# Cross-attention and experts on one core: own pair buffers, x normalized in place, expert rows turned by DMA, and a new order on every engine

## The chip, the cores and the metric

The kernel runs on one core of a Trainium2 chip. The metric is the device time of one execution in microseconds; three runs were made before the change (1605.39 median, 1598.07 to 1605.72), and one more execution was taken with the hardware profiler.

## The reference

There are 32 batches of 128 tokens with 512 features. Each batch is normalized, goes through an attention of 32 heads of 16 features, and is added to its input. The result is normalized again and goes through a layer of 8 experts, of which each token takes the best two.

```python
# attention, per batch; adapter = ctx_2048[b], also 128 rows
h = layernorm(x)
q, k, v = split_heads(h @ Wq), split_heads(h @ Wk), split_heads(h @ Wv)
q, k = rope(q), rope(k)
w = softmax(q @ k.T / 4 + mask);  o = w @ v                      # 'own' path
a_k, a_v = split_heads(adapter @ Wk), split_heads(adapter @ Wv)
o += tanh(gate) * softmax(q @ a_k.T / 4) @ a_v                   # 'adapter' path
x = x + o @ Wo
# experts, over all 4096 tokens; H = 512, I = 352, E = 8, K = 2
h = layernorm(x)
topk_vals, topk_idx = top_k(h @ router_w.T, 2);  weight = softmax(topk_vals)
gate, up = split(h[rows of e] @ w1[e].T);  y = (silu(gate) * up) @ w2[e].T
x = x + sum over the two experts of weight * y
```

## The kernel before

The program has two phases with a barrier between them. Each engine runs its own list of instructions in order and waits on semaphores. There is no scheduler at run time. The order on each engine is written out by hand in a function `step(i)`, which `walk` calls for i = 0, 1, 2 and so on (L247); `run(task, i - 5, ...)` does the task for batch i - 5. A larger number taken from i means an older batch, and only the order in which an engine meets its tasks matters.

**Number format.** Matmul operands are pairs of float16 numbers, a high and a low part: a tile is copied to float16 on ScalarE (`x_high`, `out_hi`, `h_high`, `q_high` and so on), and the rest is taken by a subtraction on GpSimd or VectorE (`x_low`, `out_low`, `h_low`). A projection (`project`, L1005) is 12 matmuls of 512 columns.

**Attention phase (L102 to L1184).** A batch passes these tasks:
- SP loads x into `xin` (`load_x`); VectorE takes its statistics (`stats_x`), GpSimd the root (`x_scale`), VectorE normalizes `xin` into `nat` (`norm_x`). ScalarE and GpSimd split `nat` into the pair `xcs`, and SP turns it into `xT` by a DMA transpose (`turn_x`). `load_x` of the next batch waits for `norm_x`.
- TensorE projects q, k and v from `xT`, and the adapter's k and v (`ak`, `avp`) from `cT`. Two PSUM banks `ma[0]`, `ma[1]` take all these results, and those of `out_project`, `router`, `places` and the turned maxima; `home` (L190) says which group uses which bank, and `latest` makes each group wait for the last reader of its bank. The router's result is in bank 0.
- q and k are rotated (VectorE), split, and turned by SP in two halves each into a ring `qkk` (`turn_q`, `turn_k`, `turn_ak`).
- `direct(n, o, path)`: scores of eight heads with queries in rows, on top of a mask that ScalarE has written into PSUM (`seed_direct`); `maxima` on VectorE takes their maximum. When all eight are there, the maxima are negated and split into three parts (`neg_max`, `neg_rest`), turned on TensorE (`max_turn`) and copied (`turned_max`).
- `scores_T(n, w)`: the same scores the other way round, on top of `seed_turned`, less the maxima; ScalarE takes exps (`exps`) into a single buffer `pr`; `values(n, w)` multiplies with v. `values_T` and `values_back` turn the sums back, `normal` (VectorE) and `paths_added` (GpSimd) divide, gate and add them into `on`.
- `out_hi` and `out_low` split `on` into the pair buffer `ohs`; SP turns it (`turn_out`), TensorE projects (`out_project`), VectorE adds the input (`residual`), and `stats_h`, `h_scale`, `norm_h` normalize it into `hn`. `h_high` and `h_low` split `hn` into the same buffer `ohs`, which SP turns (`turn_h`) and stores to `h2_pairs` (`store_h`). So `h_high` waits for the turn of the attention result of its batch, and `out_hi` for the turn and the store of h of the batch before (L653, L654, L659).
- `router`, `router_top`, `router_pick`, `places`, `router_counts`, `router_weights`, `router_rows` choose the experts; `enter_lists` scatters each token's number and weight into a list per expert.
- One slice of w1 per batch is loaded, scaled and split (`w_slice`, `w_low`). For the last batch, SP loads w2 of three experts (`load_first_w2`, six DMAs of 512 and 192 KB) ahead of `turn_out`.

**Expert phase (L1187 to L1452).** Each expert's list is cut into tiles of 128 rows; 71 slots hold them all. Per slot s: SP loads the list rows (`lrow`), GpSimd gathers the rows of h into `hg` (two buffers) by an indirect DMA, TensorE turns them in eight transposes into the PSUM tile `px` (`turn_rows`), ScalarE copies `px` to `hgT` (`rows_turned`, L1321). Then come two products of 12 matmuls (`inner`, gate and up), silu and product on ScalarE and VectorE, the split, six transposes (`turn_inner`) with copies on VectorE (L1384, L1385), nine matmuls (`outer`), a scaled copy to `yo` (`expert_out`, L1350), and an indirect DMA that adds the rows to the output in memory (`add_rows`). An `add_rows` waits for the landing of the one before (L1297). GpSimd issues `gather(s)` and then `add_rows(s - 3)`. TensorE's step s is `inner(s, 0)`, `turn_inner(s - 1)`, `inner(s, 1)`, `turn_rows(s + 1)`, `outer(s - 1)`. In the first step it waits for all of w2, whose last four experts SP loads after the list rows of slot 2 (L1273).

Of the kernel before, what the change touches and what calls it, by code (L numbers as in the profile page):

```python
# [101 lines left out]
def attention_phase(nc, ctx, dram, keep):  # L102
# [55 lines left out]
    nat = sb("nat", [P, D], F32)  # L158
# [3 lines left out]
    ohs = sb("ohs", [P, 2, D], F16)  # L162
# [27 lines left out]
    home = dict(q=0, k=1, ak=0, v=1, avp=0, o=0, router=0, places=1, mturn=1)  # L190
# [56 lines left out]
    def walk(step):  # L247
        for i in range(NB + 9):
            step(i)
# [31 lines left out]
    def _(sp):  # L281
        def load_x(n):
            source = dram["x"](n)
            sp.wait_ge(x_n.sem, x_n.at(n.shift(-1)))
            sp.dma_start(xin[:, :], source).then_inc(x_in.sem(n), 16)
# [22 lines left out]
        def store_out(n):  # L308
            sp.wait_ge(x_2.sem, x_2.at(n))
            sp.dma_start(dram["out"](n), x2[:, :]).then_inc(out_st.sem(n), 16)  # L310

        def store_h(n):
            sp.wait_ge(h_lo.sem, h_lo.at(n))
            sp.dma_start(dram["h2"](n), rows(ohs)).then_inc(h2_st.sem(n), 16)
# [15 lines left out]
        def turn_out(n):  # L330
            if n.n == NB - 1:
                load_first_w2(n)
            sp.wait_ge(o_lo.sem, o_lo.at(n))
            sp.wait_ge(o_p.sem, o_p.at(n.shift(-1)))
            sp.dma_start_transpose(turned(oT), rows(ohs)).then_inc(o_T.sem, 16)

        def turn_h(n):
            sp.wait_ge(h_lo.sem, h_lo.at(n))
            sp.wait_ge(r_p.sem, r_p.at(n.shift(-1)))
            sp.dma_start_transpose(turned(hT), rows(ohs)).then_inc(h_T.sem, 16)  # L340
# [62 lines left out]
        def step(i):  # L403
            run(turn_x, i - 2)
            run(turn_q, i - 3, 0)
            run(turn_k, i - 3, 0)
            run(turn_ak, i - 3, 0)
            run(load_residual, i - 5)
            run(turn_h, i - 6)
            run(store_h, i - 6)  # L410
            run(turn_k, i - 3, 1)
            run(next_x, i)
            run(turn_q, i - 3, 1)
            run(turn_ak, i - 3, 1)
            run(next_c, i - 1)
            run(turn_out, i - 5)
            run(next_w, i)
            run(store_out, i - 6)
            run(next_m, i - 2)
# [7 lines left out]
    def _(pool):  # L427
# [39 lines left out]
        def x_low(n):  # L467
            pool.wait_ge(x_hi.sem, x_hi.at(n))
            pool.tensor_tensor(xcs[:, 1, :], nat[:, :], xcs[:, 0, :], ALU.subtract).then_inc(x_lo.sem, 1)
# [24 lines left out]
        def out_low(n):  # L494
            pool.wait_ge(o_hi.sem, o_hi.at(n))
            pool.tensor_tensor(ohs[:, 1, :], on[:, :], ohs[:, 0, :], ALU.subtract).then_inc(o_lo.sem, 1)
# [43 lines left out]
        def step(i):  # L540
            run(h_scale, i - 7)
            run(paths_added, i - 6, 2)
            run(paths_added, i - 6, 3)
            run(w_low, i - 2)
            run(ctx_lo, i - 3)
            run(q_sum, i - 3)
            run(out_low, i - 6)
            run(x_low, i - 2)
            run(paths_added, i - 5, 0)
            run(enter_lists, i - 8)  # L550
            run(k_sum, i - 3)
            run(q_low, i - 3)
            run(paths_added, i - 5, 1)
            run(k_low, i - 3)
            run(x_scale, i - 1)
# [6 lines left out]
    def _(act):  # L562
        def x_high(n):
            act.wait_ge(x_n.sem, x_n.at(n))
            act.wait_ge(x_T.sem, x_T.at(n.shift(-1)))
            act.activation(xcs[:, 0, :], nat[:, :], ACT.Copy).then_inc(x_hi.sem, 1)
# [99 lines left out]
        def step(i):  # L666
            run(exps, i - 7, 7)
            run(values_T, i - 7, 3)
            run(own_values, i - 5)
            run(seed_turned, i - 6, 0)  # L670
            run(seed_direct, i - 5, 0)
            run(adapter_values, i - 5)
            run(exps, i - 6, 0)
            run(h_high, i - 8)
            run(w_slice, i - 3)
# [5 lines left out]
            run(out_hi, i - 7)  # L681
# [859 lines left out]
```

## Time and profile before

| | |
|---|---|
| median of three runs | 1605.39 us (1598.07 to 1605.72) |
| the profiled execution | 1610.79 us, span 1609.0 us |
| TensorE matmuls, busy | 1437.7 us, 89% of the span |
| VectorE / ScalarE / GpSimd, busy | 63% / 63% / 52% |
| mean granted clock of TensorE | 0.963 of full |

Times in rows are microseconds from the start of the span. A matmul's duration includes its pipeline, so consecutive groups overlap; the distance from start to start is what a group costs. In square brackets stands the idle time of the engine ahead of an instruction and what ended it.

### The profile page before, as it was taken

The page shows a single profiled execution, that of the slowest core. Times are in us where ns is not written, and L with a number is a line of the kernel's source. Part 1 is how long each engine was busy: PE and PEld are TensorE (multiplying, and loading weights), DVE is VectorE, ACT ScalarE, POOL GpSimd, SP SyncE. Part 2 cuts the span into 40 slices and gives each one's busy share as a digit, 9 for nine tenths or more (in the row PEclk, how much of TensorE's full clock was granted, in tenths as well). Part 3 has the DMA queues.
Part 4 walks back from the last instruction along what each step waited for, and adds up shares of the span by engine and source line. Part 5 has one row for each costly group of instructions (what it writes and reads, how often), then busy time and mean ns, then how long its engine had stood idle before and what let it go on. Part 6 is the DMA issues. An engine that isn't in the chain of part 4 may idle for free. (4 is left out here: it accounts for less than half of the span.)

```text
span 1609.0 us, 46292 instructions
## 1 busy us (share of the span) xinstructions
PE 1437.7 (89%) x16909; PEld 844.2 (52%) x16910; DVE 1017.6 (63%) x2595; ACT 1013.2 (63%) x1332; POOL 829.3 (52%) x991
## 2 busy tenths in 40 slices
PE   3899779999999999999999999861699999999996
PEld 1355445555555555555555555530366666666663
DVE  5557768888888888888888888744433332333332
ACT  4578657878878887887887888741444344344342
POOL 5445645566566566556656655421344544444443
PEclk9999979999999999999999999985799999999998
DMA  5466868677777778768767786533354454454543
GB/s 188 99 122 131 99 98 129 134 145 129 131 138 135 134 130 150 132 127 151 127 141 132 144 134 113 100 77 82 111 85 87 79 87 82 80 89 79 84 86 52
DMA packets 368118, 183.19 MB, mean 114 GB/s; under 512 B 323216, under 2 KB 327312, under 8 KB 367440
## 3 DMA queue, kind: packets, MB, share of 16 engines
q1 hardware_dynamic: 349808, 143.59, 48.2%
q0 software_dynamic: 18144, 37.31, 13.4%
q8 instruction: 114, 1.87, 0.5%
q14 instruction: 52, 0.43, 0.1%
HBM read 69.61 MB, written 35.72 MB: 65 GB/s over the span
## 5 line engine op out<-in xcount | busy, mean ns | idle before, releaser
L779 DVE TENSOR_REDUCE mx<-md 128x8 f32<-128x1024 f32 x256 | 312.9, 1222 | 106.6 <-PE md L1062 100.3
L638 ACT ACTIVATE pr<-st 128x1024 f32<-128x1024 f32 x256 | 262.0, 1023 | 172.2 <-PE st L1092 137.7
L1407 PE MATMUL y<-w1s,hgT 128*128 x1704 | 281.8, 316 | 3.3 <-ACT hgT L1321 3.3
L1407 PEld LDWEIGHTS y<-w1s,hgT 128*128 128x128 f16 x1704 | 165.1, 99 | 96.1 <-issue 3.7
L1107 PE MATMUL av<-pr,vv 128*17 128x128 f32 x4096 | 164.4, 279 | 28.5 <-ACT pr L638 28.3
L1321 ACT ACTIVATE hgT<-px 128x1024 f16<-128x1024 f16 x71 | 72.7, 1024 | 155.4 <-PE px L1397 155.4
L1426 PE MATMUL y<-w2s,yT 128*128 (+1 forms) x639 | 150.3, 379 | 0.9 <-DVE yT L1385 0.9
L503 POOL TENSOR_TENSOR part<-part,tg_r 128x128 f32<-128x128 f32 x128 | 58.3, 456 | 172.2 <-DVE part L815 168.3
L1107 PEld LDWEIGHTS av<-pr,vv 128*17 128x17 f32 x4096 | 90.9, 97 | 94.2 <-ACT pr L638 43.8
L607 ACT ACTIVATE md<-msk 128x1024 f32<-128x1024 f32 x128 | 131.0, 1023 | 10.0 <-DVE mx L779 10.0
L1384 DVE COPY yT<-py 128x256 f16<-128x256 f16 x142 | 40.4, 284 | 149.9 <-PE py L1416 149.9
L615 ACT ACTIVATE st<-msk 128x1024 f32<-128x1024 f32 x128 | 132.0, 1031 | 2.1
L1087 PE MATMUL st<-qkk 64*128 64x128 f16 x2048 | 102.3, 220 | 26.4 <-DVE mT L805 23.0
L1299 POOL TENSOR_TENSOR held<-held 128x1 f32<-128x1 f32 x71 | 13.6, 192 | 215.2 <-ACT yo L1350 211.8
L1300 POOL DMA_INDIRECT out<-yo,dst x71 | 113.5, 1599 | 16.8 <-issue 12.2
L1062 PE MATMUL md<-qkk 64*128 64x128 f16 x2048 | 101.5, 219 | 12.6 <-ACT md L607 4.8
L1092 PE MATMUL st<-mT,hsel 64*128 64x128 bf16 x2048 | 100.9, 219 | 0.0
L1008 PE MATMUL ma<-w_o,oT 128*128 128x512 f16 x384 | 91.0, 388 | 10.7 <-DMA oT<-ohs 10.7
L1008 PE MATMUL ma<-w_v,cT 128*128 128x512 f16 x384 | 93.1, 394 | 5.4 <-issue 3.7
L1008 PE MATMUL ma<-w_q,xT 128*128 128x512 f16 x384 | 91.5, 389 | 6.9 <-DMA xT<-xcs 6.9
L644 ACT ACTIVATE avT<-av 128x512 f32<-128x512 f32 x128 | 76.0, 594 | 28.6 <-PE av L1107 28.6
L1008 PE MATMUL ma<-w_k,cT 128*128 128x512 f16 x384 | 88.4, 380 | 5.7 <-DVE lg L847 3.8
(190 smaller groups left out, 2849.1 us busy)
## 6 DMA issues: line engine op xcount, KB each, us to landing
wst<-in_w SPq DMA_DIRECT2D x32, 352.0 KB, 4.0
xin<-in_x SPq DMA_DIRECT2D x32, 256.0 KB, 3.2
cin<-in_ctx SPq DMA_DIRECT2D x32, 256.0 KB
xres<-in_x SPq DMA_DIRECT2D x32, 256.0 KB, 3.0
h_pairs<-ohs SPq DMA_DIRECT2D x32, 256.0 KB, 2.3
out<-x SPq DMA_DIRECT2D x32, 256.0 KB
msk<-in_mask SPq DMA_DIRECT2D x32, 128.0 KB
lrow<-lists SPq DMA_DIRECT2D x71, 1.0 KB, 3.5
```

What stands on the lines that cost most here:

```text
L607: act.activation(md[:, :, :, :].rearrange("p r j n -> p (r j) n"), msk[:, n.par, 0, :].unsqueeze(1).to_broadcast([P, 8, P]), ACT.Copy).the ...
L615: act.activation(st[:, :, :, :].rearrange("p r j n -> p (r j) n"), msk[:, n.par, 1, :].unsqueeze(1).to_broadcast([P, 8, P]), ACT.Copy).the ...
L638: act.activation(pr[:, :, :, :], st[:, :, :, :], ACT.Exp).then_inc(p_ex.sem, 1)
L779: dve.tensor_reduce(mx[:, 2 * path:2 * path + 2, 4 * o:4 * o + 4], md[:, :, :, :], AX.X, ALU.max).then_inc(d_max.sem, 1)
L1008: i = pe.matmul(bank[:, 0:cols], xt[:, a, c, :], w[:, c, z, :], start=(n == 0), stop=(n == 11))
L1062: i = pe.matmul(md[:, r, j, :], qkk[rows, 0, slot, j, :], qkk[rows, 1 + path, slot, j, :], start=(path == 1 and j == 0), stop=(j == 3), sk ...
L1087: pe.matmul(st[:, r, j, :], qkk[rows, 1 + path, slot, j, :], qkk[rows, 0, slot, j, :], start=(path == 1 and j == 0), stop=False, skip_grou ...
L1092: i = pe.matmul(st[:, r, j, :], hsel[rows, p:p + 1].to_broadcast([64, P]), mT[rows, n.par, path, :], start=False, stop=(j == 3), skip_grou ...
L1107: i = pe.matmul(av[o % 2][VC * j:VC * j + VW, 2 * path + r, :], vv[:, n.par, path, 8 * o + 2 * j + r, :], pr[:, r, j, :], start=True, stop ...
L1300: pool.indirect_dma_start(out=dram["out_rows"], out_offset=bass.IndirectOffsetOnAxis(ap=dst[:, s.off % LB:s.off % LB + 1], axis=0), in_=yo ...
L1407: i = pe.matmul(y1[s.par][j][:, 0:F], hgT[:, s.par, a, c, :], w, start=(n == 0), stop=(n == 11))
L1426: i = pe.matmul(y2[s.par][:, :], yT[0:fn, a, k, :], w, start=(n == 0), stop=(n == 8))
```

## The change

It has six parts.

1. The attention result and h get a pair buffer each (`os`, `hs`). `out_hi` waits only for the turn of its own buffer a batch earlier, `h_high` for the turn and the store of h a batch earlier.
2. x is normalized in place in `xin`; `nat` is gone. `norm_x` waits for nothing but the root, and `load_x` waits for `x_low` of the batch before.
3. `load_first_w2` follows `store_out` of batch 30 in place of preceding `turn_out` of batch 31.
4. The router's result moves to bank 1, with the waits for it in `latest`.
5. In the expert phase `hg` and `hgT` have four buffers, and SP turns the rows by DMA transposes; TensorE's `turn_rows`, `px` and ScalarE's copies are gone. `add_rows` lags five slots. The second half of w2 follows the turn of slot 0.
6. All five engines have new orders in the attention phase.

```diff
-    ohs = sb("ohs", [P, 2, D], F16)
+    os = sb("os", [P, 2, D], F16)
+    hs = sb("hs", [P, 2, D], F16)
-    home = dict(q=0, k=1, ak=0, v=1, avp=0, o=0, router=0, places=1, mturn=1)
+    home = dict(q=0, k=1, ak=0, v=1, avp=0, o=0, router=1, places=1, mturn=1)
...
         def load_x(n):
-            sp.wait_ge(x_n.sem, x_n.at(n.shift(-1)))
+            sp.wait_ge(x_lo.sem, x_lo.at(n.shift(-1)))
...
         def store_out(n):
             sp.wait_ge(x_2.sem, x_2.at(n))
             sp.dma_start(dram["out"](n), x2[:, :]).then_inc(out_st.sem(n), 16)
+            if n.n == NB - 2:
+                load_first_w2(LAST)
...
         def out_hi(n):
             act.wait_ge(n_o.sem, n_o.at(n))
+            act.wait_ge(o_T.sem, o_T.at(n.shift(-1)))
+            act.activation(os[:, 0, :], on[:, :], ACT.Copy).then_inc(o_hi.sem, 1)
+        def h_high(n):
+            act.wait_ge(h_n.sem, h_n.at(n))
             act.wait_ge(h_T.sem, h_T.at(n.shift(-1)))
             act.wait_ge(h2_st.sem(n.shift(-1)), h2_st.at(n.shift(-1)))
-            act.activation(ohs[:, 0, :], on[:, :], ACT.Copy).then_inc(o_hi.sem, 1)
-        def h_high(n):
-            act.wait_ge(h_n.sem, h_n.at(n))
-            act.wait_ge(o_T.sem, o_T.at(n))
-            act.activation(ohs[:, 0, :], hn[:, :], ACT.Copy).then_inc(h_hi.sem, 1)
+            act.activation(hs[:, 0, :], hn[:, :], ACT.Copy).then_inc(h_hi.sem, 1)
...
         def norm_x(n):
             dve.wait_ge(x_rs.sem, x_rs.at(n))
-            dve.wait_ge(x_hi.sem, x_hi.at(n.shift(-1)))
-            dve.wait_ge(x_lo.sem, x_lo.at(n.shift(-1)))
-            dve.tensor_scalar(nat[:, :], xin[:, :], mv[:, 0, 0:1], mv[:, 0, 3:4], ALU.subtract,
+            dve.tensor_scalar(xin[:, :], xin[:, :], mv[:, 0, 0:1], mv[:, 0, 3:4], ALU.subtract,
...
         def k(n):
-            latest(pe, n, (f_cnt, -5), (m_T, -2), (v_v, -1), (k_t, -1))
+            latest(pe, n, (r_lg, -4), (f_cnt, -5), (m_T, -2), (v_v, -1), (k_t, -1))
...
         def ak(n):
-            latest(pe, n, (r_lg, -4), (q_t, 0), (av_v, -1), (x_2, -4), (ak_lo, -1))
+            latest(pe, n, (q_t, 0), (av_v, -1), (x_2, -4), (ak_lo, -1))
...
 # expert phase, SP
         def step(s, is_first, is_last):
...
             sp.wait_ge(w_row.sem, w_row.at(s.shift(-LB)))
-            sp.wait_ge(g_in.sem(s), g_in.at(s.shift(-LB)))
+            if s.off >= 2:
+                sp.wait_ge(g_in.sem(s.shift(-2)), g_in.at(s.shift(-2)))
             sp.dma_start(lrow[:, s.off % LB, :], source).then_inc(l_in.sem(s), 16)
+            if s.off >= 2:
+                turn_rows(s.shift(-2))
             if isinstance(s.n, int) and s.n == 2:
                 load_last_w2()
+            if is_last:
+                for k in (-1, 0):
+                    sp.wait_ge(g_in.sem(s.shift(k)), g_in.at(s.shift(k)))
+                    sp.wait_ge(up_p.sem, up_p.at(s.shift(k - LB)))
+                    turn_rows(s.shift(k))
+        def turn_rows(s):
+            sp.dma_start_transpose(hgT[:, s.off % LB, :, :, :].rearrange("p a c n -> p (a c) n"),
+                                   hg[:, s.off % LB, :, :].rearrange("p a n -> p (a n)")).then_inc(g_T.sem(s), 16)
...
 # expert phase, GpSimd
         def step(s, is_first, is_last):
             gather(s)
-            if s.off >= 3:
-                add_rows(s.shift(-3))
+            if s.off >= 5:
+                add_rows(s.shift(-5))
...
 # expert phase, TensorE
         def inner(s, j, e):
             if j == 0:
-                pe.wait_ge(g_T.sem, g_T.at(s))
+                pe.wait_ge(g_T.sem(s), g_T.at(s))
...
         def step(s, is_first, is_last):
...
             inner(s, 1, e)
-            if not is_last:
-                turn_rows(s.shift(1))
```

The new orders of the attention phase, one engine after the other (each line is a `run(...)`; the old orders stand in the code above):

```
SP:      turn_x -7 | store_out -11 | next_x -6 | turn_h -11 | load_residual -10 | turn_q 1 -8 | turn_k 1 -8 | next_c -6 |
         turn_ak 1 -8 | turn_out -10 | next_w -6 | store_h -11 | next_m -7 | turn_q 0 -7 | turn_k 0 -7 | turn_ak 0 -7
GpSimd:  q_sum -2 | out_low -5 | paths_added 0 -4 | enter_lists -7 | k_sum -2 | q_low -2 | paths_added 1 -4 | k_low -2 |
         x_low -1 | h_scale -5 | paths_added 2 -4 | w_low -1 | ctx_lo -1 | x_scale 0 | paths_added 3 -4
ScalarE: exps 6 -7 | seed_direct 3 -6 | router_exp -9 | exps 7 -7 | own_values -5 | values_T 3 -7 | seed_direct 0 -5 |
         seed_turned 0 -6 | h_high -8 | adapter_values -5 | exps 0 -6 | w_slice -4 | ctx_hi -4 | exps 1 -6 |
         seed_turned 1 -6 | seed_direct 1 -5 | values_T 0 -6 | exps 2 -6 | exps 3 -6 | seed_turned 2 -6 | out_hi -7 |
         values_T 1 -6 | exps 4 -6 | q_high -4 | seed_direct 2 -5 | ak_high -4 | exps 5 -6 | x_high -3 |
         seed_turned 3 -6 | k_high -4 | values_T 2 -6
VectorE: maxima 1,1 -5 | rotate_k -4 | norm_x -3 | normal 1 -6 | router_top -8 | maxima 2,0 -5 | ak_low -4 |
         router_pick -8 | maxima 2,1 -5 | residual -7 | maxima 3,0 -5 | stats_h -7 | maxima 3,1 -5 | neg_max -5 |
         neg_rest -5 | norm_h -7 | turned_max -5 | maxima 0,0 -4 | normal 2 -6 | h_low -7 | maxima 0,1 -4 | normal 3 -6 |
         router_counts -8 | router_weights -8 | router_rows -8 | router_logits -7 | stats_x -2 | rotate_q -3 |
         maxima 1,0 -4 | normal 0 -5
TensorE: scores_T 3 -7 | values 2 -7 | k -5 | values 3 -7 | direct 1,1 -6 | scores_T 4 -7 | ak -5 | values_back 1 -7 |
         values 4 -7 | scores_T 5 -7 | direct 2,0 -6 | v -5 | values 5 -7 | direct 2,1 -6 | scores_T 6 -7 |
         out_project -8 | scores_T 7 -7 | direct 3,0 -6 | values 6 -7 | values_back 2 -7 | direct 3,1 -6 | values 7 -7 |
         avp -5 | max_turn -6 | direct 0,0 -5 | scores_T 0 -6 | values_back 3 -7 | direct 0,1 -5 | places -9 |
         scores_T 1 -6 | values 0 -6 | q -4 | values 1 -6 | scores_T 2 -6 | direct 1,0 -5 | values_back 0 -6 | router -8
```

## Rows read from the trace of the kernel before

**Rows 1.** Page, part 2: TensorE's busy tenths in 40 equal slices of the span.

```profile
PE   3899779999999999999999999861699999999996
```

**Rows 2.** Timeline, 1300 to 1320 us: start, duration, engine, line, operation, operands, count.

```profile
1302.26 1.96 PE L1407 MATMUL y<-w1s,hgT 128*128 x12
...
1305.32 0.15 DVE L1370 SCALAR_TENSOR_TENSOR wrow<-lrow,wst 128x1 f32<-128x1 f32 x1
...
1306.18 0.61 PE L1397 MATMUL px<-ident,hg 128*128 128x128 f16 x8
...
1306.62 2.12 PE L1426 MATMUL y<-w2s,yT 128*128 x9
...
1308.58 1.95 PE L1407 MATMUL y<-w1s,hgT 128*128 x12
```

**Rows 3.** Timeline of TensorE, 500 to 570 us, in the steady part of attention.

```profile
522.48 0.39 PE L1087 MATMUL st<-qkk 64*128 64x128 f16 x8
522.70 0.39 PE L1092 MATMUL st<-mT,hsel 64*128 64x128 bf16 x8
523.02 0.63 PE L1107 MATMUL av<-pr,vv 128*17 128x128 f32 x16
...
524.86 0.63 PE L1107 MATMUL av<-pr,vv 128*17 128x128 f32 x16 [0.29 <-ACT pr L638]
...
528.68 0.40 PE L1087 MATMUL st<-qkk 64*128 64x128 f16 x8 [0.39 <-DVE mT L805]
...
530.45 0.63 PE L1107 MATMUL av<-pr,vv 128*17 128x128 f32 x16 [0.29 <-ACT pr L638]
...
532.02 2.76 PE L1008 MATMUL ma<-w_q,xT 128*128 128x512 f16 x12
...
562.94 2.76 PE L1008 MATMUL ma<-w_q,xT 128*128 128x512 f16 x12
```

**Rows 4.** Timeline, 1078 to 1160 us: the last batch's attention result and its projection.

```profile
1080.72 0.45 POOL L510 TENSOR_TENSOR on<-part 128x128 f32<-128x128 f32 x1
...
1083.40 0.63 ACT L655 ACTIVATE ohs<-on 128x512 f16<-128x512 f32 x1 [4.87 <-DMA h_pairs<-ohs]
...
1085.29 1.74 SPq L335 DMA_TRANSPOSE oT<-ohs  x1
...
1092.16 5.30 PE L1008 MATMUL ma<-w_o,oT 128*128 128x512 f16 x12 [9.30 <-DMA oT<-ohs]
```

**Rows 5.** The chain that ended last, in order of time: start, duration, what.

```profile
1130.12 7.29 DMA hg<-h_pairs,lrow
```

**Rows 6.** Line 347, 300 to 1000 us: landing of the DMA transposes of q, k, ak.

```profile
DMA to landing us min/median/max: 3.0/3.3/5.5
```

**Rows 7.** Page, part 6: gathers, count and median time to landing.

```profile
hg<-h_pairs,lrow POOLq DMA_INDIRECT x71, 4.2
```

**Rows 8.** Line 1300, 1160 to 1590 us: landing of the scatter-adds.

```profile
DMA to landing us min/median/max: 4.7/4.9/5.6
```

**Rows 9.** DMA queues, 500 to 900 us (q1) and 1160 to 1560 us (q0): packets, MB, engine share.

```profile
q1 hardware_dynamic: 135409, 53.59, 74.5%
...
q0 software_dynamic: 14154, 33.12, 47.8%
```

**Rows 10.** Timeline, 1136 to 1175 us: end of w2's conversion and slot 1's product.

```profile
1147.42 0.68 DVE L1361 SCALAR_TENSOR_TENSOR w2s<-w2f,w2s 96x512 f16<-96x512 f32 x1
...
1148.95 3.54 PE L1407 MATMUL y<-w1s,hgT 128*128 x12 [2.09 <-ACT hgT L1321]
```

**Rows 11.** Waits of TensorE in the whole span: us in total, times, longest.

```profile
PE ma L1008 <- DVE lg L847: 3.8, 4, 1.4
```

**Rows 12.** Timeline of VectorE, 500 to 533 us: stats_h and the next copy.

```profile
527.22 0.69 DVE L827 BATCH_NORM_STATS2 stat<-x 128x6 f32<-128x512 f32 x1
...
528.33 0.29 DVE L805 COPY mT<-ma 128x256 bf16<-128x256 bf16 x1
```

**Rows 13.** Timeline of ScalarE, 500 to 533 us: exps 0.

```profile
529.37 1.02 ACT L638 ACTIVATE pr<-st 128x1024 f32<-128x1024 f32 x1 [0.35 <-PE st L1092]
```

More of the change, by code:

```diff
@@ L247, in walk @@
     def walk(step):
-        for i in range(NB + 9):
+        for i in range(NB + 11):
             step(i)
@@ L339, in turn_h @@
             sp.wait_ge(r_p.sem, r_p.at(n.shift(-1)))
-            sp.dma_start_transpose(turned(hT), rows(ohs)).then_inc(h_T.sem, 16)
+            sp.dma_start_transpose(turned(hT), rows(hs)).then_inc(h_T.sem, 16)
         def turn_half(n, h, plane, src, split, done):
@@ L403, in step @@
         def step(i):
[L404 to L419, printed above, removed]
+            run(turn_x, i - 7)
+            run(store_out, i - 11)
+            run(next_x, i - 6)
+            run(turn_h, i - 11)
+            run(load_residual, i - 10)
+            run(turn_q, i - 8, 1)
+            run(turn_k, i - 8, 1)
+            run(next_c, i - 6)
+            run(turn_ak, i - 8, 1)
+            run(turn_out, i - 10)
+            run(next_w, i - 6)
+            run(store_h, i - 11)
+            run(next_m, i - 7)
+            run(turn_q, i - 7, 0)
+            run(turn_k, i - 7, 0)
+            run(turn_ak, i - 7, 0)
         walk(step)
@@ L666, in step @@
         def step(i):
+            run(exps, i - 7, 6)
+            run(seed_direct, i - 6, 3)
+            run(router_exp, i - 9)
             run(exps, i - 7, 7)
+            run(own_values, i - 5)
             run(values_T, i - 7, 3)
-            run(own_values, i - 5)
+            run(seed_direct, i - 5, 0)
             run(seed_turned, i - 6, 0)
-            run(seed_direct, i - 5, 0)
+            run(h_high, i - 8)
             run(adapter_values, i - 5)
             run(exps, i - 6, 0)
-            run(h_high, i - 8)
-            run(w_slice, i - 3)
+            run(w_slice, i - 4)
+            run(ctx_hi, i - 4)
             run(exps, i - 6, 1)
@@ L1145, in step @@
         def step(i):
+            run(scores_T, i - 7, 3)
+            run(values, i - 7, 2)
+            run(k, i - 5)
+            run(values, i - 7, 3)
+            run(direct, i - 6, 1, 1)
+            run(scores_T, i - 7, 4)
+            run(ak, i - 5)
+            run(values_back, i - 7, 1)
+            run(values, i - 7, 4)
+            run(scores_T, i - 7, 5)
+            run(direct, i - 6, 2, 0)
+            run(v, i - 5)
+            run(values, i - 7, 5)
+            run(direct, i - 6, 2, 1)
@@ new lines, in step @@
+            run(scores_T, i - 7, 6)
+            run(out_project, i - 8)
+            run(scores_T, i - 7, 7)
+            run(direct, i - 6, 3, 0)
+            run(values, i - 7, 6)
+            run(values_back, i - 7, 2)
+            run(direct, i - 6, 3, 1)
+            run(values, i - 7, 7)
+            run(avp, i - 5)
+            run(max_turn, i - 6)
+            run(direct, i - 5, 0, 0)
+            run(scores_T, i - 6, 0)
+            run(values_back, i - 7, 3)
+            run(direct, i - 5, 0, 1)
```

216 lines of the change are left out of this document (81 added, 135 removed).

## The prediction

> **What bounds the kernel now.** First the slices: TensorE is full over two long stretches, with a valley of some 90 us between them [rows 1]. The first stretch is attention, 32 batches; the second the experts, 71 slots. So I read each from TensorE's own timeline.
>
> In the expert stretch TensorE never waits: one slot runs from 1302.26 to 1308.58, 6.32 us, and between the second inner product and the outer one stand the eight transposes of the next slot's rows, 1306.18 to 1306.62: 0.44 us [rows 2]. Whatever leaves TensorE there shortens the slot, until another chain is longer. In attention a batch takes 30.92 us (projections at 532.02 and 562.94), with three waits in it, 0.29 + 0.39 + 0.29 = 0.97 us [rows 3]. In the valley TensorE waits for the last turn of the attention result [rows 4], then for the first gathered rows [rows 5].
>
> **The change part by part.** The sum is made against the profiled execution, 1610.79 us (span 1609.0, 1.8 around it). It is 5.4 above the median, 1605.39; I carry the difference over to the median.
>
> *Transposes of expert rows.* 71 groups of eight leave TensorE, and as many copies (L1321) leave ScalarE. The first group stands before the steady slots; 70 x 0.44 = **-30.8 us**. The slot would be 5.88. Does each other chain fit?
> - The turned rows. SP issues turn_rows(s+2) behind lrow(s+4), which waits for w_row(s). That instruction ran 3.1 us into its slot (1305.32 against 1302.26) [rows 2]. With some 0.9 us for the two issues the DMA starts 4.0 into the slot. Turns of the same size landed 3.0/3.3/5.5 us (least, median, most) after issue in attention [rows 6], so at worst at 9.5, and the rows are needed at 11.8: slack 2.3. The gather is no later: lrow(s+4) lands about 7 into slot s, the gather follows and takes 4.2 [rows 7], some 13 in all, and the turn that needs it goes at 11.8 + 4.0 = 15.8. Behind a waiting turn_rows on SP stands only the next lrow, with the same slack.
> - The scatter-adds. Each waits for the landing of the last: 4.9 us (4.7 to 5.6) from its issue [rows 8]. With about 0.35 for the held instruction and the issue this chain takes 5.25 per slot. It fits under 5.88 with 0.6 to spare; that is the thinnest place. Add_rows now lags five slots in place of three and stands behind the gather on GpSimd, which costs nothing in itself: an add must be down before the output four slots later.
> - The DMA engines. In 400 us of attention, 13 batches, SP's queue takes 74.5% of the 16 engines and moves 53.59 MB [rows 9]: 298 us. Were all of it the nine turns per batch, one would take 298 / 117 = 2.55 us; at the same cost per byte as the rest (0.262 MB each) 1.46. I take 1.8, nearer to the lower, since the turns carry over half of the bytes. In the expert stretch GpSimd's queue takes 47.8% of 6.32, 3.0 us [rows 9]. Sum 4.8 of 5.88 us, 82% (4.5 to 5.6): full, but not over.
> - The inner chain: VectorE's copies for the outer product are done before 1305.32; the product started at 1306.62 [rows 2] and moves 0.44 ahead. Hidden.
>
> The Trainium skill speaks against this edit ("VectorE: DVE Perf Modes", The three transpose paths, and Rules for kernel authors): it prefers TensorE for a 128x128 transpose and gives 1.309 us for one by DMA. The trace's DMA turns hold eight such blocks and land in 3.3 us together [rows 6]; the measurement decides.
>
> *Start of the experts.* Before, the second half of w2 went out before the first gather landed, and that gather took 7.29 us [rows 5] against 4.2 usual [rows 7]. Now SP waits for gather 0, turns it, and only then loads w2. The first inner product comes about 1.5 us sooner, but w2's eight issues come some 9 us later, and TensorE may not leave slot 0 without all of w2. Its last instruction began at 1147.42, and slot 1's product at 1148.95 behind the copy of its rows [rows 10]: there is 1 us of cover. ScalarE used to break off the conversion for the row copy and needs no longer, so I count about half of the 9 us; turn_rows(1) queues behind 2.8 MB besides. Bounds 0 (conversions keep up) and +9; I take **+3.5**.
>
> *w2's first loads* (six issues, 0.33 to 0.65 us each) move from ahead of turn_out(31) to behind store_out(30), past turn_h(30) and load_residual(31) on SP. Before, on(31) was complete at 1081.2, but ScalarE waited until 1083.40 (4.87 us idle) for the store of h before it could write the shared ohs; the turn went out at 1085.29, and the projection started at 1092.16 after 9.30 us of waiting [rows 4]. With own buffers the turn can go at 1083.1. The loads start some 6 us sooner and drain sooner; turn_h(30) now lies behind them and lands about 1087, and router(30) stands ahead of the projection on TensorE. So the projection starts about 1088: **-4 us** (-7 to 0).
>
> *Own buffers and x in place, in the steady batches.* The waits removed (ScalarE for h's turn and store, VectorE for x_high and x_low) are on no wait of TensorE [rows 3]: 0. The added wait of load_x for x_low sits on SP right behind turn_x, which has waited for the same event: 0. The load then has most of a batch until stats_x. Without that cover it would cost its landing, some 3 us a batch.
>
> *Router to bank 1.* ak's wait for lg goes, 3.8 us in the whole run [rows 11]: **-3.8**. k takes it over; VectorE's copy comes about 0.8 us before k in the new order. Without that cover up to the same 3.8 comes back.
>
> *New orders in attention.* I lay TensorE's new order out with the old spacings. A 64-row group followed by its like takes 0.22 us, followed by another shape 0.32 (522.48, 522.70, 523.02) [rows 3]. The new order has two more such changes (28 for 26): +0.2 per batch. The waits:
> - values 7 for exps 7 (0.29) stays: the same two groups lie between.
> - scores 0 for the turned maximum (0.39): direct 0 now lies between, which alone would leave 0.15. But its seed on ScalarE comes ahead of the turned seed and waits for the last maximum, and stats_h, 1.1 us (527.22 to the next copy at 528.33) [rows 12], now stands before that maximum. I get 0.2.
> - values 0 for exps 0 (0.29) becomes a wait of scores 1 for exps 0. ScalarE had 0.35 us to spare there [rows 13]; h_high, about 0.6, now stands before it: 0.25. Direct 0,1 waits another 0.15 for its maximum, and values_back 0 waits 0.2 behind ScalarE's w_slice, ctx_hi, exps and two seeds.
>
> That is 1.1 against 0.97. In all +0.2 to +0.3; I take 0.2 x 28 batches = **+5.6**. A few tenths of slack on three engines decide it: bounds -0.5 and +0.6 per batch, -14 to +17. SP's new order puts three turns of q, k, ak ahead of turn_x: from their release to q lie 8.9 us, 3.9 of issue, so the landing may take 5.0; at most it took 5.5 [rows 6]. That is inside the bounds.
>
> The first two batches: x_high stands ahead of w_slice, so the first turn goes some 2 us sooner, but norm_x(1) stands behind the weights: -1 (bounds -5 and +3).
>
> Sum: -30.8 + 3.5 - 4 - 3.8 + 5.6 - 1 = **-30.5**: 1580.3 on the profiled execution's scale, 1574.9 on the median's; I say 1576.
>
> **The rivals.**
> 1. *The new orders gain.* For: direct 0 fills most of 0.39, and the bank waits go. Against: stats_h and h_high land on the path. At -0.5 per batch instead of +0.2: 20 us less, 1556.
> 2. *The new orders eat the gain.* For: after the last maximum VectorE's chain has only 0.1 us in hand before the turn on TensorE, and x's turn has 5 us. Against: SP's queue is empty at that point. A further 0.9 us per batch is +25: 1601, no change.
> 3. *The scatter-adds become the bound* (slower). Place: the add's landing, with a turn and a gather now in the same part of the slot. From a landing of 5.97 us the slot is 6.32 again, 1606. With the whole 1.8 us of the turn on top of 4.9 the slot is 7.05: 71 x 0.73 = +52, with the other terms 1657. For: engines at 82%, the largest landing already 5.6. Against: an add that slips falls behind the turn and the gather, where the engines are free.
> 4. *Turns too slow for a slot.* If turns ran in series at more than 5.88 us each, the slot would be theirs. Against: 5.5 at most, with other traffic [rows 6]. Even 6.5 would give 71 x 0.18 = +13, 1618. By the skill's time above, as an estimate from that page, eight blocks in series would take 10.5 us a slot, +297.
>
> That the transposes do not leave TensorE can't be: its step has none left.
>
> **How the numbers follow.** Forecast 0.62, rival 1 0.18, rival 2 0.10, rival 3 0.09 (0.04 around 1606, 0.05 slower), rival 4 0.01. The low end is rival 1 and a little more, 1554; the high end takes in rival 2 and the first part of rival 3, 1606. The likeliest case's own range is 1564 to 1590. 0.5%, 8 us, is about what a measurement of this kernel can tell from no change: faster is below 1597, slower above 1613. Faster 0.62 + 0.18 + a fifth of rival 2 = 0.82; same, the rest of it and a part of rival 3, 0.11; slower 0.07.
>
> **What would show it.** Slots of 5.88 us with no wait of TensorE in them; adds landing under 5.5 us and turns under 7; slot 1 some 3 us later behind its first product; the last projection's wait near 5; batches of 31.1 us, with waits at scores 0 and scores 1. The prediction is wrong if the slot exceeds 6.1 or the batch 31.8.

## The result: slower, 1641.65 us for 1604.18

The changed kernel takes 1641.65 us (median of four runs, 1632.63 to 1645.92), the kernel before it 1604.18 in the same comparison: ratio 1.023, 95% interval 1.0201 to 1.026. The forecast was 1576. The profiled execution of the changed kernel took 1632.63 us, with a span of 1630.9 against 1609.0.

The difference of the spans, +21.9 us, splits at six places that both traces have:

| stretch | before | after | difference |
| --- | --- | --- | --- |
| start to the last q projection | 996.70 | 1047.08 | +50.4 |
| from there to the last output projection | 95.46 | 91.36 | -4.1 |
| to the first inner product of slot 1 | 56.79 | 59.51 | +2.7 |
| to the outer product of slot 0 | 6.05 | 6.67 | +0.6 |
| to the outer product of slot 70 | 438.92 | 408.55 | -30.4 |
| to the end | 15.08 | 17.73 | +2.7 |

The split holds for these two executions. The medians lie 37.5 us apart: the changed kernel's profiled execution is the fastest of its four, that of the kernel before is slower than all four of its own, and the traces don't show where the other 15.6 us lie.

The main row, TensorE's last projection of q, before and after:

```profile
996.70 2.76 PE L1008 MATMUL ma<-w_q,xT 128*128 128x512 f16 x12
```

```profile
1047.08 2.76 PE L1006 MATMUL ma<-w_q,xT 128*128 128x512 f16 x12
```

The expert phase gives what was forecast; attention loses 50 us. The slices show the same, TensorE of the changed kernel (answers to [rows 1]):

```profile
PE   4899889998999989998999999985079999999995
```

Over the steady part it stands at 8 and 9 where the row of before had nines throughout. The clock has no part in it: from 216 to 990 us the granted clock is 1.00 of full in both traces.

**The expert slot** (timeline of the changed kernel, all engines, about 1300 us; answers to [rows 2]):

```profile
1300.52 1.95 PE L1399 MATMUL y<-w1s,hgT 128*128 x12
...
1304.43 2.12 PE L1418 MATMUL y<-w2s,yT 128*128 x9
...
1306.39 1.95 PE L1399 MATMUL y<-w1s,hgT 128*128 x12
```

5.87 us from slot to slot, with no wait of TensorE; the outer product follows the inner one directly. The turns of the rows land a little sooner than those of attention did (line 1283, 1210 to 1610 us; answers to [rows 6]):

```profile
DMA to landing us min/median/max: 2.8/2.8/5.9
```

**A steady batch of attention** (timeline of TensorE in the changed kernel: every wait of 0.2 us or more between two projections of q; answers to [rows 3]):

```profile
682.26 2.76 PE L1006 MATMUL ma<-w_q,xT 128*128 128x512 f16 x12
...
700.73 0.40 PE L1060 MATMUL md<-qkk 64*128 64x128 f16 x8 [0.41 <-DVE mx L777]
...
702.02 2.75 PE L1006 MATMUL ma<-w_o,oT 128*128 128x512 f16 x12 [0.44 <-DVE aks L741]
...
706.14 0.40 PE L1060 MATMUL md<-qkk 64*128 64x128 f16 x8 [0.82 <-ACT md L607]
...
707.89 0.40 PE L1060 MATMUL md<-qkk 64*128 64x128 f16 x8 [0.20 <-DVE mx L777]
...
715.18 2.76 PE L1006 MATMUL ma<-w_q,xT 128*128 128x512 f16 x12
```

32.92 us for 30.92 [rows 3]. The waits that were foreseen (values 7, scores 0, scores 1) are not among them. The new ones all hang on one stretch of VectorE: the two maxima of group 2 (L777) with ak_low (L741) between them. Why these come late is seen in VectorE, GpSimd and ScalarE side by side (timeline of the changed kernel, 694 to 706 us):

```profile
696.13 1.29 POOL L487 TENSOR_TENSOR t<-t 128x512 f32<-128x512 f32 x1
...
696.61 2.94 DVE L853 TENSOR_TENSOR gap<-top 128x1 f32<-128x1 f32 x1
696.68 0.39 PE L1060 MATMUL md<-qkk 64*128 64x128 f16 x8
697.36 2.16 POOL L483 TENSOR_TENSOR qs<-t,qs 128x1024 f16<-128x1024 f32 x1
...
699.46 1.21 DVE L777 TENSOR_REDUCE mx<-md 128x8 f32<-128x1024 f32 x1
...
700.42 2.13 POOL L492 TENSOR_TENSOR ks<-t,ks 128x1024 f16<-128x1024 f32 x1
...
702.05 0.53 DVE L860 CAST chosen_at<-first 128x2 f32<-128x2 uint32 x1
702.51 1.15 POOL L469 TENSOR_TENSOR xcs<-xin,xcs 128x512 f16<-128x512 f32 x1
702.61 1.08 DVE L862 TENSOR_TENSOR oh<-iota,chosen_at 128x16 f32<-128x16 f32 x1
...
703.81 1.22 DVE L777 TENSOR_REDUCE mx<-md 128x8 f32<-128x1024 f32 x1
...
705.06 1.03 ACT L607 ACTIVATE md<-msk 128x1024 f32<-128x1024 f32 x1 [2.40 <-DVE mx L777]
```

router_top's subtraction of one number per partition (gap, L853) takes 2.94 us. It ends at 699.55, within 0.03 us of GpSimd's q_low (697.36 + 2.16 = 699.52). The scores for the first maximum of group 2 were there by 697.1 (PE, 696.68 + 0.39), but the maximum starts at 699.46. In router_pick the cast ends 0.03 us behind k_low, and the one-hot row 0.03 us behind x_low. The second maximum therefore ends at 705.03; ScalarE's seed for group 3, idle for 2.40 us, starts then, and TensorE behind it.

### The profile page after: what moved, and what is told of

It reads as the page before. It is cut to its first block and busy times, and to the rows that moved or that the text cites. A ratio compares the mean times of both kernels' runs of the same rounds, so it can differ in the third digit from the quotient of the medians.

```text
span 1630.9 us, 44982 instructions
## 1 busy us (share of the span) xinstructions
PE 1430.8 (88%) x16341; PEld 816.1 (50%) x16342; DVE 1062.2 (65%) x2595; ACT 952.2 (58%) x1261; POOL 832.2 (51%) x991
## 5 line engine op out<-in xcount | busy, mean ns | idle before, releaser
L777 DVE TENSOR_REDUCE mx<-md 128x8 f32<-128x1024 f32 x256 | 312.2, 1219 | 78.9 <-PE md L1060 69.6
L1060 PE MATMUL md<-qkk 64*128 64x128 f16 x2048 | 102.5, 220 | 59.8 <-ACT md L607 31.8
L503 POOL TENSOR_TENSOR part<-part,tg_r 128x128 f32<-128x128 f32 x128 | 63.0, 492 | 158.4 <-DVE part L813 158.3
L1339 ACT ACTIVATE yp<-ya 128x352 f16<-128x352 f32 x71 | 35.2, 496 | 162.4 <-DVE ya L1377 162.4
L1060 PEld LDWEIGHTS md<-qkk 64*128 64x128 f16 x2048 | 60.7, 95 | 101.1 <-DVE mx L777 45.2
L525 POOL TENSOR_TENSOR mv<-mv,mhalf 128x1 f32<-128x1 f32 x32 | 18.1, 567 | 165.7 <-DVE mv L830 165.7
L1418 PEld LDWEIGHTS y<-w2s,yT 128*128 128x128 f16 (+1 forms) x639 | 62.3, 97 | 67.7 <-issue 1.1
```

Of the source, the lines that this page charges most:

```text
L777: dve.tensor_reduce(mx[:, 2 * path:2 * path + 2, 4 * o:4 * o + 4], md[:, :, :, :], AX.X, ALU.max).then_inc(d_max.sem, 1)
L1060: i = pe.matmul(md[:, r, j, :], qkk[rows, 0, slot, j, :], qkk[rows, 1 + path, slot, j, :], start=(path == 1 and j == 0), stop=(j == 3), sk ...
L1418: i = pe.matmul(y2[s.par][:, :], yT[0:fn, a, k, :], w, start=(n == 0), stop=(n == 8))
```

## Theories and experiments

- **Theory A.** Small VectorE instructions with two SBUF inputs stand still while GpSimd runs a tensor instruction. The new order puts router_top and router_pick, beside k_sum, q_low and k_low, ahead of the maxima that TensorE needs next.
- **Rival B.** The new place of these steps costs, however long they take.
- **Rival C.** Another part (own buffers, x in place, loads, turns, the router's bank) makes the batch longer.

**x1_gap: the changed kernel, one instruction in another form.**

```diff
-dve.tensor_tensor(gap[:, 0:1], top[:, 1:2], top[:, 0:1], ALU.subtract)
+dve.tensor_scalar(gap[:, 0:1], top[:, 1:2], top[:, 0:1], None, ALU.subtract)
```

> The changed kernel with one instruction of the router in another form: the gap of the two largest logits as a tensor_scalar with a per-partition scalar in place of a tensor_tensor with two SBUF inputs (same values, same place in VectorE's order). Theory A (the router's small two-input instructions on VectorE stand still while a GpSimd instruction runs; in the new order that is k_sum and q_low, and the maximum of group 2 stands behind them): the gap takes 0.15 us in place of a median of 2.92, the batch falls from 33.2 to about 31.5 us, the run to 1590 to 1600 us. Rival B (the new place of router_top in VectorE's order costs, whatever the instruction takes): the gap gets short but the batch stays at 32.7 us or more, the run at 1628 or more. Rival C (another part of the change makes the batch longer: the buffers, the loads, the DMA turns): the same, batch 33.2, run 1641.

Measured 1578.52 us (ratio to before 0.986, 0.9828 to 0.9892): 63 us below the changed kernel. Line 853 from 100 to 1040 us, first in the changed kernel, then in this one (duration in ns least/median/most, first and last start):

```profile
L853 DVE TENSOR_TENSOR gap<-top x27: 160/2922/3195, 150.6 to 1028.5; 128x1 f32<-128x1 f32 x27
```

```profile
L853 DVE TENSOR_SCALAR gap<-top x29: 212/214/215, 151.5 to 1033.2; 128x1 f32<-128x1 f32 x29
```

Batches 7 to 31 take 31.12 us on average, for 33.34 in the changed kernel and 31.22 before. The instruction stands at the same place and every other part of the change is in, so B and C fall. It gained more than A expected: 2.2 us per batch for 1.7, and a run below the 1590 to 1600 of its range. A part of that may be router_pick, which now starts sooner and falls beside other instructions of GpSimd: its one-hot row has a median of 0.18 us here for 1.08 in the changed kernel.

**x8_qlow: the gap as it was, GpSimd's instruction cut.**

```diff
-pool.tensor_tensor(qs[:, :, 2:4, :], twice(t1), qs[:, :, 0:2, :], ALU.subtract)
+pool.tensor_tensor(qs[:, 0:1, 2:4, :], twice(t1)[:, 0:1, :, :], qs[:, 0:1, 0:2, :], ALU.subtract)
```

> The changed kernel with one GpSimd instruction cut down: q_low computes the low half of q for head 0 alone (128x32 in place of 128x1024; the rest of the low half stays zero, so this part of the computation is left out). VectorE's gap stays a tensor_tensor at its place. Theory A (GpSimd's running instruction holds VectorE's two-input instruction): the gap ends with k_sum, 0.9 us after its start in place of 2.9 (up to 1.9 if it must also let the short instructions behind k_sum pass), batch 31.2 to 32.2 us, run 1580 to 1612. Rival (the tensor_tensor form is slow at this place for a reason on VectorE itself): gap 2.9 us, batch 33.2, run 1641.

Measured 1578.68 us (0.9828, 0.9794 to 0.9862). Timeline of this run, GpSimd and VectorE:

```profile
661.28 1.28 POOL L489 TENSOR_TENSOR t<-t 128x512 f32<-128x512 f32 x1
661.75 0.83 DVE L855 TENSOR_TENSOR gap<-top 128x1 f32<-128x1 f32 x1
662.51 0.24 POOL L484 TENSOR_TENSOR qs<-t,qs 128x32 f16<-128x32 f32 x1
```

The same tensor_tensor ends at 662.58, 0.02 us behind k_sum (662.56). So GpSimd's running instruction is what holds it, as A says. The two runs name the same cause from both sides and give the same time.

**x4_top: the two steps at another place.**

```diff
 run(router_logits, i - 7)
+run(router_top, i - 7)
+run(router_pick, i - 7)      # and gone from ahead of the maxima of group 2
```

> The changed kernel with router_top and router_pick moved on VectorE to right behind the copy of the logits, one batch-step sooner (all else as changed). There GpSimd ran nothing for about 1 us, and VectorE waited 1.57 us for the logits. Theory A: the gap takes 0.16 us and the pick about 0.7 in all, the maximum of group 2 starts 3 to 4 us sooner after rotate_k; rotate_q starts 1 to 1.4 us later, which gives a part back: batch 31.3 to 32.2, run 1585 to 1612. Rival B expects the same of this run, rival C 1641.

Measured 1593.62 us (0.994, 0.9921 to 0.9959). With the old form, where GpSimd is idle:

```profile
L853 DVE TENSOR_TENSOR gap<-top x28: 158/159/163, 141.7 to 1013.0; 128x1 f32<-128x1 f32 x28
```

The hold is gone, the batch's floor (its shortest batches) is 31.45 us: 1.5 of the 2.0 us come back. The other 0.5 goes where the expectation has it. The maximum behind rotate_q ends later, and in each of batches 7 to 31 TensorE waits 0.5 to 0.6 us for it, a wait that isn't in x1_gap (timeline of TensorE in this run):

```profile
669.16 0.40 PE L1060 MATMUL md<-qkk 64*128 64x128 f16 x8 [0.60 <-DVE mx L777]
```

At the changed order's place with a form that isn't held the kernel is 15 us faster than this.

**b_gap: the kernel before, with the same one instruction changed** (the diff of the first run, on the other kernel).

> The kernel before with the same one instruction in the other form: the gap as a tensor_scalar. There the held tensor_tensor took a median of 0.63 us, and VectorE waited 0.32 us more for the next scores afterwards. Theory A (a hold costs only where the order has no slack behind it): 0.21 us, batch 31.1 as before, run within 5 us of the kernel before. Rival (the form of the instruction itself is worth time in any order, by the 0.4 us): 0.4 x 28 = 11 us faster.

Measured 1604.55 us (1.0013, 0.9998 to 1.0027). Line 855 from 100 to 1000 us in the kernel before, then here:

```profile
L855 DVE TENSOR_TENSOR gap<-top x27: 159/625/633, 145.7 to 978.2; 128x1 f32<-128x1 f32 x27
```

```profile
L855 DVE TENSOR_SCALAR gap<-top x27: 212/213/216, 147.3 to 974.7; 128x1 f32<-128x1 f32 x27
```

The old order held it too, for 0.4 us, and had slack there. Worth nothing in one order, the edit is worth 63 us in the other.

**x2_orders: the old orders with the other parts of the change.**

```diff
+run(turn_x, i - 2); run(next_x, i - 1)     # SP; all else in the five orders as before
-home = dict(..., router=1, ...)
+home = dict(..., router=0, ...)
```

> The changed kernel with the attention orders of all five engines and the router's bank as before; own buffers for the attention result and h, x normalized in place (x's load stands right behind x's turn on SP) and the whole expert phase stay as changed. Theory A and rival B (the orders cost): batches of 31.2 us again, the whole about 1575 us (1604 less 27 to 30). Rival C (buffers, x in place, loads): batch 32 us or more, whole above 1600.

Measured 1718.64 us (1.0737, 1.069 to 1.0785). By the letter that is rival C's "above 1600", but it is far above what any theory priced: the run doesn't tell them apart, for it brings a wait of its own. Waits of VectorE in this run (us in total, times, longest):

```profile
DVE stat L706 <- DMA xin<-in_x: 134.7, 31, 10.4
```

With x normalized in place its load can go only behind x_low, and the old order asks for x's statistics too soon after that: 4.3 us of waiting in each of 31 batches; batches 7 to 31 take 36.3 us on average. The granted clock is lower there too, 0.92 of full from 216 to 990 us where it is 1.00 before, and how the 5 us a batch divide between the two wasn't tested. So x in place needs the new order's later stats_x, or it brings this wait. Whether the own buffers alone would do with the old orders wasn't tried.

**x3_expert and x10_old: the expert phase alone, on the kernel before; the second also loads w2 sooner.**

```diff
+if isinstance(s.n, int) and s.n == 2: load_last_w2()     # x10_old
 if s.off >= 2: sp.wait_ge(g_in.sem(s.shift(-2)), g_in.at(s.shift(-2)))
 ...
-if isinstance(s.n, int) and s.n == 2: load_last_w2()     # x10_old
```

> The kernel before with the expert phase of the change alone (rows turned by DMAs, four row buffers, the last w2 loads behind the second slot's turn, adds five slots late); attention untouched. Every theory: slots of 5.87 us in place of 6.32, -31 over 70 slots; the start of the experts gives back 3 to 4 us; 1575 to 1579. Rival (DMA turns or scatter-adds get in each other's way): above 1590.

> The orders of before throughout attention, with the expert phase of the change and the second half of w2 loaded ahead of SP's wait for the first gathered rows. If the new orders, mended, are worth no more than the old ones (batches of 31.1 us in both): 1571 to 1576, the same as the mended change with that load (1575). If they are worth the waits they remove (0.5 to 0.6 us per batch, 14 to 17 us): 1585 or more.

Measured 1576.93 us (0.9833, 0.9801 to 0.9865) and 1572.85 us (0.9827, 0.9813 to 0.9842). The expert phase of the change carries the whole gain; the own buffers, x in place and the new orders, mended, add nothing that these runs can tell. Both kinds of order have batches of 31.1 us on average. The mended new one (x1_gap) has fewer listed waits of TensorE, 0.5 us a batch for 1.1, but the rest of its batch is as much longer.

**x6_pick, x5_w2 and x9_both: on x1_gap, the pick in single-input forms, w2 loaded sooner, and both.**

```diff
-dve.tensor_tensor(oh[:, :, :], iota8 (both rows), chosen_at (both columns), ALU.is_equal)
+dve.tensor_scalar(oh[:, 0, :], iota8[:, :], chosen_at[:, 0:1], None, ALU.is_equal)     # and row 1
-dve.tensor_tensor(sel[:, :], oh[:, 0, :], oh[:, 1, :], ALU.add)
+dve.tensor_reduce(sel[:, :], oh[:, :, :].rearrange("p a e -> p e a"), AX.X, ALU.add)
```

> The run with the gap as tensor_scalar (1578.5 us), with the pick's two held instructions in single-input forms as well: the one-hot rows as two tensor_scalars with a per-partition scalar, their sum as a tensor_reduce over two columns. In that run the one-hot row took 0.48 us and the sum 2.13, standing still during k_low, ahead of the second maximum of group 2. Theory A: 0.3 and 0.17 us; that maximum 2 us sooner, the wait of direct 3,0 (0.48 us) and of direct 3,1 (0.20) gone: batch 30.2 to 30.5 us for 30.9, run 1558 to 1570. Rival (a tensor_scalar of eight columns is held like a tensor_tensor): the one-hot rows take 0.5 to 1.5 us, the sum 0.17 to 1; run 1570 to 1579.

> The run with the gap as tensor_scalar (1578.5 us), with the second half of w2 loaded ahead of SP's wait for the first gathered rows in place of behind it. Theory (in the change these loads came too late and slot 1 waits for their conversion, 8.12 us): the loads start 9 to 5 us sooner, the last conversion ends about 1131 in place of 1138.8; the first gather lands 2 to 3 us later beside them, first product at 1128 for 1125.6; slot 1's product 4 to 5 us sooner, run 1573 to 1575. Rival (the gather loses as much to the loads as the conversions gain): 1577 to 1580.

> Both edits on the run with the gap as tensor_scalar: the pick in single-input forms and the second half of w2 loaded ahead of the wait. Theory A and the w2 theory: the sum of the two, 1554 to 1566 us, some 40 to 50 below the kernel before and 77 to 87 below the changed one. If the rivals hold: 1572 to 1579.

Measured 1575.76 us (0.9795, 0.9753 to 0.9837), 1575.10 (0.9793, 0.9764 to 0.9823) and 1576.21 (0.9807, 0.9776 to 0.9838): apart from each other, and from x10_old, by less than their intervals. x6_pick and x9_both miss what A expected. The sum isn't held any more, but the batch's floor stays at 30.86 us, where it was in x1_gap; once the gap is short, the pick's holds aren't what sets the batch. The expectation had also taken one batch for all: in x1_gap the sum takes 2.13 us in five of the 28 batches between 216 and 1040 us, and its median is 0.31 (line 867 there):

```profile
L867 DVE TENSOR_TENSOR sel<-oh x27: 166/310/2133, 155.1 to 977.8; 128x8 bf16<-128x8 f32 x27
```

The one-hot row shows which forms are held (timeline of x6_pick):

```profile
670.23 0.46 POOL L510 TENSOR_TENSOR on<-part 128x128 f32<-128x128 f32 x1
670.24 0.48 DVE L862 TENSOR_SCALAR oh<-iota,chosen_at 128x8 f32<-128x8 f32 x1
...
670.72 2.13 POOL L492 TENSOR_TENSOR ks<-t,ks 128x1024 f16<-128x1024 f32 x1
...
670.89 0.17 DVE L867 TENSOR_REDUCE sel<-oh 128x8 bf16<-128x16 f32 x1
```

A tensor_scalar of eight columns waits for GpSimd as well (0.48, to 0.03 us behind its end); the tensor_reduce goes through in the middle of k_low. In x1_gap the sum, as a tensor_tensor, takes the whole of k_low where it is held longest:

```profile
666.73 2.13 POOL L492 TENSOR_TENSOR ks<-t,ks 128x1024 f16<-128x1024 f32 x1
666.76 2.13 DVE L867 TENSOR_TENSOR sel<-oh 128x8 bf16<-128x8 f32 x1
```

Loading w2 sooner works through another balance than expected: TensorE in x1_gap, then in x5_w2, at the start of the experts:

```profile
1125.59 5.96 PE L1399 MATMUL y<-w1s,hgT 128*128 x24 [29.09 <-DMA hgT<-hg]
1139.67 3.70 PE L1399 MATMUL y<-w1s,hgT 128*128 x12 [8.12 <-DVE w2s L1361]
...
1145.58 2.12 PE L1418 MATMUL y<-w2s,yT 128*128 x9
```

```profile
1137.70 7.32 PE L1399 MATMUL y<-w1s,hgT 128*128 x36 [34.19 <-DMA hgT<-hg]
...
1147.20 2.12 PE L1418 MATMUL y<-w2s,yT 128*128 x9
```

Counted from the last q projection (990.84 and 996.21) the first product comes 6.7 us later, not 2 to 3; slot 1's wait for w2 is gone, and the first outer product comes 3.75 us sooner. On the way stands a hold again, the other way round (timeline of x5_w2):

```profile
1122.24 0.68 DVE L1361 SCALAR_TENSOR_TENSOR w2s<-w_k,w2s 96x512 f16<-96x512 f32 x1
1122.47 3.37 POOL L1296 TENSOR_TENSOR held<-held 128x1 f32<-128x1 f32 x1 [14.04 <-DMA lrow<-lists]
...
1126.00 1.27 POOL L1297 DMA_INDIRECT hg<-h_pairs,lrow  x1
```

GpSimd's one-number instruction ahead of the first gather takes 3.37 us for 0.19, while VectorE converts w2 in one instruction after another. But this isn't what made the 6.7 us. In x1_gap the same conversions fell on the gather's own issue, 4.13 us for 0.97:

```profile
1115.54 4.13 POOL L1297 DMA_INDIRECT hg<-h_pairs,lrow  x1
```

From the start of the one-number instruction to the end of the issue it is 4.5 us in x1_gap and 4.8 in x5_w2. Of the 6.7 us, 1.9 lie ahead of that (1.6 of them already when the expert phase begins), and 4.6 in the landing: from the end of its issue the gather lands in 2.4 us in x1_gap and in 7.0 in x5_w2, where w2's loads are under way.

**x11_hold and x12_hold_new: on x10_old and x5_w2, VectorE's conversion waits for the first gather.**

```diff
 for e in range(NE):
+    if e == 1:
+        dve.wait_ge(gather_held.sem, gather_held.at(Batch(0, 1, LB)))
     dve.wait_ge(w2_hi.sem, w2_hi.at(Batch(0, 0), 2 * e + 2))
```

> The old orders with the changed expert phase and the early w2 loads (1572.85 us), with one wait added: VectorE converts the first expert's w2 and then waits until GpSimd has issued the first gather (its second held instruction). Theory (the hold works both ways: in the changed order with early loads GpSimd's held instruction ahead of the first gather took 3.37 us in place of 0.19, to the end of VectorE's conversions): the held instruction takes at most 1.5 us, the gather goes 3 us sooner and shares less with w2's loads, which start some 3 us later; the first product comes 3 to 5 us sooner, counted from the last q projection, and the run takes 1568 to 1570 us. Rival (the 3.4 us are the landing of the list, or something else that this wait doesn't touch): held instruction 3.4 us as before, run 1573 to 1577, since the conversions come later.

> The same added wait on the new orders with the gap in its other form and the early w2 loads (1575.1 us). Theory: first product 3 to 5 us sooner, counted from the last q projection (141.5 us there), run 1570 to 1572. Rival: 1575 to 1579.

Measured 1580.18 us (0.9826, 0.9799 to 0.9853) and 1575.84 (0.9802, 0.9771 to 0.9833): no gain, though the mechanism is as the theory has it. Timeline of x12_hold_new:

```profile
1123.26 0.19 POOL L1296 TENSOR_TENSOR held<-held 128x1 f32<-128x1 f32 x1 [13.70 <-DMA lrow<-lists]
1123.60 0.99 POOL L1297 DMA_INDIRECT hg<-h_pairs,lrow  x1
...
1138.30 8.28 PE L1401 MATMUL y<-w1s,hgT 128*128 x36 [33.48 <-DMA hgT<-hg]
```

The held instruction is back at 0.19 us and the gather goes 2.4 us sooner, yet the first product doesn't come sooner. SP waits for the later conversions before its last w2 load, and the first turn stands behind that load: counted from the last q projection it goes 3.2 us sooner than in x5_w2, but it lands in 6.55 us for 2.75, with w2's last load issued 1.0 us ahead of it in place of 7.9. What the gather gains, the turn loses; that the load is what slows it wasn't tested.

## Why the prediction was wrong

**The step that failed is "New orders in attention".** It put +0.2 us a batch, with bounds of -0.5 and +0.6; the traces give 33.34 - 31.22 = +2.13 a batch, +53.2 over the last 25; the start and the first six batches gave 2.8 of it back, so +50.4 in all. It laid out TensorE's order with the old spacings and counted the waits of each order by the durations that instructions had in the old one. That doesn't hold for an instruction whose duration is a wait: gap took 0.63 us at its old place and 2.92 at the new one. The steps that carry it, router_top and router_pick, now stand ahead of the two maxima of group 2, and the working gave that no price. The old trace had such rows: among the router's small instructions beside GpSimd there, chosen took 1.20 us (its like, oh, 0.18):

```profile
L917 DVE TENSOR_TENSOR chosen<-oh,pos x25: 1198/1203/1210, 224.2 to 973.1; 128x16 f32<-128x16 f32 x25
```

The step's list of waits looked at stats_h and the last maximum; the late link was the middle of VectorE's round. The limit that it gave itself (a batch over 31.8) was passed.

With the gap in its other form the forecast's time stands: 1578.5 us for 1576, and batches of 31.12 us for 31.1. Not all of its working does. The 31.1 was one steady batch of 30.92 and 0.2 more; on average the batches of before took 31.22, so the mended orders are 0.1 shorter, not 0.2 longer. Nor are there waits at scores 0 and scores 1 in x1_gap's steady batches; its 0.5 us a batch are at the products that feed the maxima. That the sum comes out so near is in part luck. Rival 2 had the direction, but another place (after the last maximum) and less than half the size.

The other steps, measured in the changed kernel:
- *Transposes of expert rows*: -30.8 forecast, -30.4 measured; slots of 5.87 for 5.88. Turns land in a median of 2.8 us, under the 3.0 that was the least in [rows 6]. The Trainium skill ("VectorE: DVE Perf Modes", Rules for kernel authors) prefers TensorE for a 128x128 transpose where PSUM will do as its destination. The measurement decided against it here: what left TensorE was 0.45 us a slot, and TensorE doesn't wait for the DMA turn in the steady slots.
- *Adds*: "0.6 to spare" was too much. They land in 4.9 us as forecast, but the chain from one to the next is some 5.7 us, because from the landing to the next issue it is 0.8 us and not 0.35. In 48 of the 71 slots GpSimd waits for the landing of the add before. They don't set the slot, but they fall behind, and the run ends on them:

```profile
1613.17 2.12 PE L1418 MATMUL y<-w2s,yT 128*128 x9 [0.93 <-DVE yT L1385]
...
1615.58 1.55 POOL L1310 DMA_INDIRECT out<-yo,dst  x1 [0.46 <-issue]
...
1621.27 1.55 POOL L1310 DMA_INDIRECT out<-yo,dst  x1 [0.46 <-issue]
```

The last add goes out 8.1 us after the last outer product's start; in the kernel before it was 5.4. That is the +2.7 at the end, a small form of rival 3 that the sum lacked. In x12_hold_new the end comes 20.1 us behind the last outer product, and the chain that ended last runs over the adds for most of the expert phase (20% of the span): this is likely to be the next limit.
- *Start of the experts*: +3.5 forecast, +2.7 and +0.6 measured. Its mechanism held: slot 1 waits 9.11 us for w2's conversion, where it waited 2.09 for its rows [rows 10].
- *w2's first loads and own buffers*: -4 forecast, -4.1 measured. The answers to [rows 4] (timeline of the changed kernel):

```profile
1130.43 0.63 ACT L654 ACTIVATE os<-on 128x512 f16<-128x512 f32 x1 [2.61 <-POOL on L510]
1132.32 1.66 SPq L335 DMA_TRANSPOSE oT<-os  x1
...
1138.44 4.59 PE L1006 MATMUL ma<-w_o,oT 128*128 128x512 f16 x12 [2.98 <-DMA oT<-os]
```

ScalarE waits for the result alone, no longer for the store of h, and the projection waits 2.98 us for 9.30. From the finished result to the projection it is 8.0 us for 11.0; so the mechanism gave 3.0 of the 4.1, and the rest lies in the steps ahead of it in that stretch, which the term didn't count.
- *Router to bank 1*: -3.8 forecast. TensorE's wait for the copy of the logits [rows 11] is gone in the changed kernel; its part of the time can't be told from that of the orders.
- *Own buffers and x in place, steady batches*: 0 forecast; x1_gap's batches, 31.12 us for 31.22, bear it out in the new orders. "Without that cover it would cost its landing, some 3 us": x2_orders took the cover away, and VectorE waited 4.3.

## What to carry to other kernels

When an order of engines is rearranged, the duration of an instruction isn't a constant to carry along: look for small rows that take far longer at one place than their shape does elsewhere, and see whose instruction ends with them. Ahead of an instruction that releases TensorE put no two-input VectorE step that may fall beside a long GpSimd one; one operand as a per-partition scalar was enough here. A large change that loses is worth taking apart before it is dropped: one instruction hid a gain of 1.4%, and the old orders with the new expert phase alone give as much.

## What the runs showed of the hardware that wasn't expected

Held by GpSimd's running tensor instruction, each to within 0.03 us of its end: tensor_tensor with both inputs in SBUF (0.16 us alone; 2.92, 1.08 and 2.13 held), a cast of two columns (0.17; 0.53), a tensor_scalar of eight columns (0.22; 0.48). Not held: tensor_scalar of one column with a per-partition scalar (0.21 us in all of 29, also beside k_sum), tensor_reduce (0.17 in the middle of k_low), and the maxima, which read PSUM (1.23 beside q_low in x1_gap). In the other direction VectorE's conversions held a GpSimd instruction (0.19; 3.37), and the issue of a gather took 4.13 us for 0.97 beside them. GpSimd didn't take longer for it (q_low 2.16 us beside the held gap, 2.14 without).

The Trainium skill has the rule ("SBUF — State Buffer", SBUF: two separate sides): VectorE and GpSimd share one pair of ports as an exclusive lock for a whole instruction, and VectorE asks for it in its two-port modes or, against a GpSimd instruction that reads SBUF, with two SBUF inputs. The rows agree, with the numbers above. By that rule the failed step could have asked what GpSimd runs beside the router in the new order.

What stays open: in the changed kernel the gap was held through two GpSimd instructions in a row, k_sum and q_low, in x8_qlow only to the end of k_sum, though the short q_low followed it directly. The runs don't show who gets the turn when both wait.
